# Experts' results: from row scatters by GpSimd to stores by SyncE and gathers by GpSimd

## The chip, the cores and the metric

The kernel runs on one core of a Trainium2 chip. A core has a matrix engine (TensorE, in the profile PE, with its weight loads as PEld), VectorE (DVE), ScalarE (ACT), GpSimd (POOL) and SyncE (SP); they work side by side, each through its own instructions in order, and wait for each other by semaphores. Sixteen DMA engines move data between HBM and the on-chip memory; DMAs are issued by SyncE and by GpSimd, and in this kernel only GpSimd issues those whose row addresses are data (indirect DMAs). The metric is the device time of one execution in microseconds (us). The median of three runs of the kernel before is 1285.11 us (1284.5 to 1285.67).

## The reference

The input is four sequences of 512 tokens of 256 values in float32: 2048 tokens, or 16 token tiles of 128. Four layers are added to it in turn, each with a layer norm in front: linear attention, a mixture of experts, softmax attention, and the same mixture of experts again.

```python
    x = x + _L0_attn_a_ref(_layernorm(x, axis=-1), ...)      # chunked linear attention, 16 heads
    x = x + _L0_ffn_ref(_layernorm(x, axis=-1), ...)         # experts, first use
    x = x + _L0_attn_b_ref(_layernorm(x, axis=-1), ...)      # softmax attention
    x = x + _L0_ffn_ref(_layernorm(x, axis=-1), ...)         # experts, second use

    def _L0_ffn_ref(hidden_states, gate_weight, gate_up_proj, down_proj):   # 32 experts, INTER = 96
        probs = softmax(x @ gate_weight.T)
        top_vals, top_idx = jax.lax.top_k(probs, TOP_K)                      # TOP_K = 8
        renorm = top_vals / sum(top_vals); cum = cumsum(renorm)
        num_keep = min(sum(cum < THRESHOLD) + 1, TOP_K)                      # THRESHOLD = 0.8
        ...                                                                  # combine: the kept shares, renormalised
        for each expert (w_gu, w_d, ce):
            g, u = split(x @ w_gu.T)
            acc = acc + (silu(g) * u) @ w_d.T * ce[:, None]
        return acc
```

Since seven of eight equal shares already pass 0.8, a token goes to at most seven experts (RANKS = 7).

## The kernel before

The work runs in four stages, one block of engine programs each: `lightning` (linear attention), `experts` with the name f, `attention`, and `experts` with the name g. Between two blocks every engine waits for the others. `X`, all 16 token tiles, stays on chip.

**Routing.** `Routing` picks the experts of each batch f of four token tiles. GpSimd then scatters the normalised rows into the HBM table `expert_rows`, sorted by expert: one indirect DMA of 128 rows for each token tile and rank, 28 for each batch (L981). A row has the 256 values, 32 shares (one for each expert) and 32 slot columns, which tell for each expert at which row of `result_rows` the token's result belongs (ROW = 320). `index` holds the row in `expert_rows` of each token and rank. The routing of the last batch, and its scatters, run inside `experts`.

**Experts.** 144 tiles of 128 rows, in 72 pairs. In each step u of the loop TensorE turns pair u (L1435), does gate and up of pair u-1 (L1447), turns the hidden values of pair u-2 (L1458) and does down of pair u-3 (L1466); ScalarE copies the result of pair u-4 to `ys` (`keep_result`, L1508). The pairs come in three phases of 24, 28 and 92 tiles (`PHASES`), each listed by VectorE once the batches that it covers are routed. SyncE reads the row addresses of pair u from the list (`rows_of`, L1368), waits until the ring of 8 input buffers has room, and issues two loads (L1390). In its passes 17 to 24 it also stores four rows-of-zeros tiles per pass (`store_pads`, L1399), and the first load of the last phase, pass 26, waits for all of them.

**Results.** VectorE takes the two slot columns of a pair out of its rows (L1531). GpSimd scatters the results of every pair to `result_rows`, which is in the order of the tokens, by one indirect DMA per tile (L1295). 22 pair buffers lie between ScalarE and these scatters. In stage f the last 11 pairs are scattered at the start of `attention`. SyncE loads the seven results of each of a token tile's 128 tokens by one plain DMA of 896 KB (`load`, L1304, ring of 2), and VectorE folds seven to one and adds it to `X` (`add`, L1312 and L1315). A token tile of the first two batches needs the first 44 pairs, one of the third 58, the others 65 or all 72 (`LOADED`). In f the sums of tiles 0 to 3 stand at steps 66 to 72, of tiles 4 to 15 in `attention`; in g all 16 stand from step 62 on, and each is followed by the store of the tile to the output.

What sets the order is the code itself: each engine's program is a loop over the steps with tables that say at which step a piece stands (`scatters_at`, `results_at`, `loads_at`, `adds_at`).

## Time and profile before

| what | us |
|---|---|
| median of three runs | 1285.11 |
| span of the profiled execution | 1109.5 |
| median less that span (start and end of the program, outside the trace) | 175.6 |
| `lightning` | 0 to 287 |
| `experts` f | 287 to 523.7 |
| `attention` | 523.7 to 829 |
| `experts` g | 829 to 1109.5 |
| busy: PE, DVE, ACT, POOL | 882.3, 583.1, 549.3, 647.3 |

The span runs from the first to the last instruction. A timeline row gives start, duration, engine, line, operation, and in brackets the idle time before it with what ended it. "issue" means that nothing in the profile was waited for. POOL's indirect DMAs count as busy while POOL writes their descriptors; a SyncE DMA only takes the time of its issue there, and its data land later.

### The profile page before, as it was taken

The page shows a single profiled execution, that of the slowest core. Times are in us where ns is not written, and L with a number is a line of the kernel's source. Part 1 is how long each engine was busy: PE and PEld are TensorE (multiplying, and loading weights), DVE is VectorE, ACT ScalarE, POOL GpSimd, SP SyncE. Part 2 cuts the span into 40 slices and gives each one's busy share as a digit, 9 for nine tenths or more (in the row PEclk, how much of TensorE's full clock was granted, in tenths as well). Part 3 has the DMA queues.
Part 4 walks back from the last instruction along what each step waited for, and adds up shares of the span by engine and source line. Part 5 has one row for each costly group of instructions (what it writes and reads, how often), then busy time and mean ns, then how long its engine had stood idle before and what let it go on. Part 6 is the DMA issues. An engine that isn't in the chain of part 4 may idle for free. (4 is left out here: it accounts for less than half of the span.)

```text
span 1109.5 us, 20646 instructions
## 1 busy us (share of the span) xinstructions
PE 882.3 (80%) x5504; PEld 667.1 (60%) x5504; DVE 583.1 (53%) x2104; ACT 549.3 (50%) x1088; POOL 647.3 (58%) x636
## 2 busy tenths in 40 slices
PE   5999998861588899997388987988658889999930
PEld 3666666541478799996243543534227778999830
DVE  4566785875364222226776587764623622222665
ACT  6333455730254455654267775775515454555520
POOL 2465658777666677776720011364655567777773
PEclk9999999995699999999679998988888999999975
DMA  9900002122649886783430011135327588767875
GB/s 343 381 4 2 1 25 84 72 84 82 196 163 306 285 263 219 221 268 131 144 133 34 34 34 44 44 113 212 112 104 238 188 282 276 233 217 249 288 244 195
DMA packets 93231, 181.64 MB, mean 164 GB/s; under 512 B 18985, under 2 KB 73788, under 8 KB 92736
## 3 DMA queue, kind: packets, MB, share of 16 engines
q1 hardware_dynamic: 68544, 114.19, 31.7%
q0 software_dynamic: 24576, 66.13, 16.3%
q8 instruction: 50, 0.82, 0.3%
q14 instruction: 61, 0.50, 0.2%
HBM read 96.34 MB, written 92.27 MB: 170 GB/s over the span
## 5 line engine op out<-in xcount | busy, mean ns | idle before, releaser
L1295 POOL DMA_INDIRECT result_rows<-ys,result_slots x288 | 291.5, 1012 | 104.1 <-issue 93.7
L981 POOL DMA_INDIRECT expert_rows<-route_rows,index x224 | 223.5, 998 | 99.8 <-issue 90.3
L1946 ACT ACTIVATE b_probs<-ps 128x1024 f32<-128x1024 f32 x128 | 127.8, 1031 | 43.9 <-PE ps L1795 43.3
L1447 PE MATMUL ps<-w_gu,g_xts 128*128 x576 | 109.1, 333 | 3.0 <-ACT g_xts L1490 2.2
L1447 PE MATMUL ps<-w_gu,f_xts 128*128 x576 | 108.6, 333 | 2.4 <-ACT f_xts L1490 1.9
L1447 PEld LDWEIGHTS ps<-w_gu,g_xts 128*128 128x128 f32 x576 | 94.6, 195 | 5.1 <-issue 4.9
L1447 PEld LDWEIGHTS ps<-w_gu,f_xts 128*128 128x128 f32 x576 | 94.5, 194 | 3.7 <-issue 3.6
L1540 DVE SCALAR_TENSOR_TENSOR f_h<-ps,f_xs,f_gate 128x96 f32<-128x96 f32 x144 | 39.2, 313 | 100.0 <-ACT f_gate L1497 98.5
L1540 DVE SCALAR_TENSOR_TENSOR g_h<-ps,g_xs,g_gate 128x96 f32<-128x96 f32 x144 | 39.0, 313 | 96.8 <-ACT g_gate L1497 89.6
L1807 PE MATMUL ps<-b_probs,b_v_pad 128*32 128x512 f32 x512 | 78.2, 686 | 11.4 <-issue 5.6
L1508 ACT COPY ys<-ps 128x512 f32<-128x512 f32 x144 | 83.6, 581 | 2.0 <-PE ps L1466 2.0
L1312 DVE TENSOR_TENSOR parts<-parts 128x768 f32<-128x768 f32 (+2 forms) x96 | 66.3, 691 | 16.8 <-DMA parts<-result_rows 14.5
L1466 PE MATMUL ps<-g_w_d,g_hts 128*128 x288 | 75.0, 384 | 0.0
L1466 PE MATMUL ps<-f_w_d,f_hts 128*128 x288 | 74.9, 384 | 0.0
L1795 PE MATMUL ps<-b_q_t,b_k_t 64*128 64x512 f32 x256 | 63.4, 523 | 13.0 <-ACT b_probs L1946 10.8
L1490 ACT COPY f_xts<-ps 128x512 f32<-128x512 f32 x72 | 42.2, 587 | 59.0 <-PE ps L1435 57.7
L373 PE MATMUL ps<-a_q_mask,a_k_t 128*128 128x512 f32 x128 | 67.2, 608 | 5.4 <-POOL a_q_mask L578 3.6
L1490 ACT COPY g_xts<-ps 128x512 f32<-128x512 f32 x72 | 42.2, 586 | 55.5 <-PE ps L1435 55.4
L1795 PEld LDWEIGHTS ps<-b_q_t,b_k_t 64*128 64x128 f32 x256 | 24.8, 200 | 57.6 <-issue 28.4
L1435 PE MATMUL ps<-ident,f_xs 128*128 128x128 f32 x288 | 45.4, 282 | 15.8 <-DMA f_xs<-expert_rows 15.8
L587 POOL TENSOR_TENSOR a_rrms<-a_ms,a_root 128x8 f32<-128x8 f32 x32 | 54.0, 1688 | 6.8 <-DVE a_ms L721 6.3
L578 POOL TENSOR_TENSOR a_q_mask<-a_q_t,a_head_rows 128x512 f32<-128x512 f32 x40 | 41.8, 1048 | 25.7 <-PE ps L373 21.7
(362 smaller groups left out, 1827.6 us busy)
## 6 DMA issues: line engine op xcount, KB each, us to landing
parts<-result_rows SPq DMA_DIRECT2D x32, 896.0 KB, 5.2
f_xs<-expert_rows SPq DMA_DIRECT2D x144, 160.0 KB
g_xs<-expert_rows SPq DMA_DIRECT2D x144, 160.0 KB
expert_rows<-pad_rows SPq DMA_DIRECT2D x64, 160.0 KB
w_gu<-in_Wgu SPq DMA_DIRECT2D x1, 6144.0 KB, 17.6
expert_rows<-pad_rows SPq DMA_DIRECT2D x1, 5120.0 KB, 39.7
result_rows<-ys,result_slots POOLq DMA_INDIRECT x288, 3.3
f_w_d<-in_Wdown SPq DMA_DIRECT2D x1, 4096.0 KB, 29.4
```

What stands on the lines that cost most here:

```text
L373: nc.tensor.matmul(ps[:, bank_s + q % 2, :], k_t[:, q // 2, n * P:(n + 1) * P], q_mask[:, q % 2, :, :], start=True, stop=True).then_inc(sc ...
L981: self.nc.gpsimd.indirect_dma_start(xs, bass.IndirectOffsetOnAxis(self.index[:, f, t, r:r + 1].bitcast(U32), 0), self.x_rows(f)[:, t, :], ...
L1295: self.nc.gpsimd.indirect_dma_start(self.y_dram, bass.IndirectOffsetOnAxis(self.slots[:, i, j:j + 1].bitcast(U32), 0), self.ys[:, i, j, :] ...
L1312: self.nc.vector.tensor_tensor(parts[:, 0:pairs, :], parts[:, 0:pairs, :], parts[:, left:left + pairs, :], ALU.add).then_inc(self.folded, 1)
L1447: ins = nc.tensor.matmul(ps[:, bank_gu[u % 2], j * GU:(j + 1) * GU], xts[:, u % 2, o:o + P], w_gu[:, k, bass.ds(experts[j] * GU, GU)], sta ...
L1466: ins = nc.tensor.matmul(ps[:, bank_y[u % 2], j * D:(j + 1) * D], hts[:, u % 2, j * P:(j + 1) * P], w_d[:, bass.ds(experts[j] * D, D)], st ...
L1490: nc.scalar.copy(xts[:, u % 2, :], ps[:, bank_x[u % 2], :]).then_inc(xt_sb, 1)
L1508: nc.scalar.copy(results.ys[:, results.at(u), :, :], ps[:, bank_y[u % 2], :].rearrange("p (j n) -> p j n", j=2)).then_inc(y_ready, 1)
L1540: ins = nc.vector.scalar_tensor_tensor(out=h[:, u % 2, j, 0:INTER], in0=up, scalar=share, in1=gate[:, u % 2, j, :], op0=ALU.mult, op1=ALU. ...
L1795: ins = nc.tensor.matmul(ps[:, 2 * (u % 2) + j, :], k_t[rows, g, st * P:(st + 1) * P], q_t[rows, 2 * g + jp, :], start=True, stop=True)
L1807: ins = nc.tensor.matmul(ps[j * PAD:(j + 1) * PAD, bank_values, :], v_pad[:, st, g, :], probs[:, (2 * i + j // 2) % RING, j % 2, :], start ...
L1946: nc.scalar.activation(probs[:, u % RING, :, :], ps[:, 2 * (u % 2):2 * (u % 2) + 2, :], ACT.Exp, scale=float(HD) ** -0.5).then_inc(exp_don ...
```

## The change

- The results of a pair no longer go to the token's row. SyncE stores each tile of results as a block, at the same row addresses at which it loaded the tile's input (`keep`): `result_rows` now has the rows of `expert_rows`. The registers with the addresses are kept from `load(u)` to `keep(u)`, which stands 9 passes later (BEHIND = 9). The result buffers are 4 pairs (`ys`, YS), and ScalarE waits for the store of pair u-4.
- GpSimd fetches the seven results of each token by their addresses in `index`: seven indirect DMAs of 128 rows for a token tile (`gather`), to a ring of 3 tile buffers (before: 2). A tile is gathered once its pairs are stored (`COMPLETE`, the same 44, 58, 65 and 72).
- In f tiles 0 to 7 are gathered and added inside `experts`, and tiles 8 to 15 inside `attention`, where before tiles 4 to 15 were added. In g all 16 are gathered from step 46 of GpSimd's program on, and added at steps 53 to 80 of VectorE's. The stores of the output stand behind all other work of SyncE.
- The slot columns go (ROW = 288), with the scan and the addition that filled them and the two casts per pair that read them.

```diff
-ROW = D + 2 * E
+ROW = D + E
...
-RESULTS = 22
-LATER = 11
-RESULTS_AT = PARTS_AT - RESULTS * 2 * D * 4
+PARTS = 3
...
+    def gather(self, pool, t):
+
+        if t >= self.RING:
+            pool.wait_ge(self.added, t - self.RING + 1)
+        for r in range(RANKS):
             self.nc.gpsimd.indirect_dma_start(
-                self.y_dram, bass.IndirectOffsetOnAxis(self.slots[:, i, j:j + 1].bitcast(U32), 0), self.ys[:, i, j, :],
-                None, bounds_check=NT * P * RANKS - 1, oob_is_err=False).then_inc(self.scattered[i], 16)
...
+                self.parts[:, t % self.RING, r, :].bitcast(I32), None, self.y_dram,
+                bass.IndirectOffsetOnAxis(self.index[:, t // TT, t % TT, r:r + 1].bitcast(U32), 0),
+                bounds_check=STORED - 1, oob_is_err=True).then_inc(self.gathered[t % self.RING], 16)
...
+            def keep(u):
+                sp.wait_ge(y_ready, u + 1)
+                for j, row in enumerate(held.pop(u)):
+                    sp.dma_start(results.y_dram[bass.ds(row, P), :],
+                                 ys[:, u % YS, j, :].bitcast(I32)).then_inc(results.stored[u % YS], 16)
...
-            for u in range(PAIRS + 6 * TT):
+            for u in range(PAIRS + BEHIND):
                 if u < PAIRS:
                     load(u)
                 if PADS_AT <= u < PADS_AT + E // PADS:
                     store_pads(PADS * (u - PADS_AT), PADS)
-                for t in loads_at(u):
-                    load_results(t)
+                if u >= BEHIND:
+                    keep(u - BEHIND)
...
             def keep_result(u):
                 act.wait_ge(down_ready, u + 1)
-                results.wait_free(act, u)
+                if u >= YS:
+                    act.wait_ge(results.stored[u % YS], 32 * (u // YS))
...
-                i = results.at(u)
-                for j in range(2):
-                    nc.vector.tensor_copy(results.slots[:, i, j:j + 1], xs[:, u % RING, j, bass.ds(experts[j] + D + E, 1)])
...
+        def gathers_at(slot, b):
+
+            tiles = {-1: {17: 8, 18: 9}, 0: {2: 10, 8: 11, 17: 12, 18: 13}, 1: {2: 14, 18: 15}}
...
-            sums = {-1: {9: 4, 16: 5, 26: 6, 30: 7}, 0: {1: 8, 3: 9, 13: 10, 28: 11}, 1: {13: 12, 23: 13, 27: 14, 31: 15}}
+            sums = {0: {1: 8, 3: 9, 13: 10, 28: 11}, 1: {13: 12, 23: 13, 27: 14, 31: 15}}
...
+        def gathers_at(u, last):
+
+            if u == COMPLETE[0] + 2:
+                yield from range(NT if last else 2 * TT)
...
-            first, count = (62, NT) if last else (66, TT)
-            at = u - first
-            if at >= 0 and at % 2 == 0 and at // 2 < count:
-                yield at // 2
+            for t in range(NT if last else 2 * TT):
+                if u == min(53 + 13 * t // 4, 80):
+                    yield t
```

GpSimd's program in `experts` f, before (L981 scatters the routed rows, L1295 the results; x116 is a run of 116 instructions):

```order
L981 DMA expert_rows<-route_rows,index 73728x320 x14
L1295 DMA result_rows<-ys,result_slots 14336x256 x2
L981 DMA expert_rows<-route_rows,index 73728x320 x2
L1295 DMA result_rows<-ys,result_slots 14336x256 x2
L981 DMA expert_rows<-route_rows,index 73728x320 x2
L1295 DMA result_rows<-ys,result_slots 14336x256 x2
L981 DMA expert_rows<-route_rows,index 73728x320 x30
L1295 DMA result_rows<-ys,result_slots 14336x256 x116
L1334 UNCONDITIONAL_BRANCH
```

The same place and the start of `attention` now (L976 scatters the routed rows, L1276 gathers the results, b_rrms is the root of the first batch's queries and keys):

```order
L976 DMA expert_rows<-route_rows,index 73728x288 x48
L1276 DMA parts<-result_rows,index 128x256 x56
L1313 UNCONDITIONAL_BRANCH
L68 ISA x2
L1929 UNCONDITIONAL_BRANCH
L797 MEMSET b_ln_root 128x4
L959 MEMSET g_route_root 128x4
L1952 MEMSET b_root 128x8
L816 TENSOR_TENSOR b_ln_rstd<-b_ln_var_eps,b_ln_root 128x4
L1954 MEMSET b_v_pad 128x512
L1936 TENSOR_TENSOR b_rrms<-b_mean_sq,b_root 128x8
L1276 DMA parts<-result_rows,index 128x256 x14
```

The 122 result scatters of the stage have become 56 gathers, all behind the 48 row scatters, and nothing stands between those any more.

GpSimd's start of `attention` before:

```order
L819 TENSOR_TENSOR b_ln_rstd<-b_ln_var_eps,b_ln_root 128x4
L1987 MEMSET b_v_pad 128x512
L1989 MEMSET b_v_pad 128x16
L1295 DMA result_rows<-ys,result_slots 14336x256 x14
L1969 TENSOR_TENSOR b_rrms<-b_mean_sq,b_root 128x8
L1295 DMA result_rows<-ys,result_slots 14336x256 x8
L819 TENSOR_TENSOR b_ln_rstd<-b_ln_var_eps,b_ln_root 128x4
```

Before, b_rrms stood behind 14 scatters; now it stands ahead of the first 14 gathers.

SyncE's program at the boundary between passes 17 and 18 of `experts` f, before (the last store of a tile of zeros, then the list and the loads of the next pair):

```order
L1399 DMA expert_rows<-pad_rows 128x320
L1368 TENSOR_LOAD tab
L1390 ISA
L1390 DMA f_xs<-expert_rows 128x320
L1390 ISA
L1390 DMA f_xs<-expert_rows 128x320
L1395 TENSOR_LOAD pads
```

and now (L1382 is the store of zeros, L1388 the new stores, L1348 and L1373 the list and the loads):

```order
L1382 DMA expert_rows<-pad_rows 128x288
L1388 ISA
L1388 DMA result_rows<-f_ys 128x256
L1388 ISA
L1388 DMA result_rows<-f_ys 128x256
L1348 TENSOR_LOAD tab
L1373 ISA
L1373 DMA f_xs<-expert_rows 128x288
L1373 ISA
L1373 DMA f_xs<-expert_rows 128x288
L1378 TENSOR_LOAD pads
```

Each pass of SyncE from 9 on has two more DMAs, in front of the next pair's loads.

## Rows read from the trace of the kernel before

**Rows 1.** The page: span, and busy time of each engine.
```profile
span 1109.5 us, 20646 instructions
PE 882.3 (80%) x5504; PEld 667.1 (60%) x5504; DVE 583.1 (53%) x2104; ACT 549.3 (50%) x1088; POOL 647.3 (58%) x636
```
**Rows 2.** Timeline of PE, experts f and g: start us, us, engine, line.
```profile
385.25 0.60 PE L1435 MATMUL ps<-ident,f_xs 128*128 128x128 f32 x4
...
444.54 0.60 PE L1435 MATMUL ps<-ident,f_xs 128*128 128x128 f32 x4
...
512.30 0.60 PE L1435 MATMUL ps<-ident,f_xs 128*128 128x128 f32 x4
...
518.20 1.97 PE L1466 MATMUL ps<-f_w_d,f_hts 128*128 x8
...
927.90 0.60 PE L1435 MATMUL ps<-ident,g_xs 128*128 128x128 f32 x4
...
987.19 0.60 PE L1435 MATMUL ps<-ident,g_xs 128*128 128x128 f32 x4
...
1062.46 1.99 PE L1466 MATMUL ps<-g_w_d,g_hts 128*128 x8
```
**Rows 3.** The page's costliest groups: line, what, count, busy, mean ns, idle before.
```profile
L1295 POOL DMA_INDIRECT result_rows<-ys,result_slots x288 | 291.5, 1012 | 104.1 <-issue 93.7
```
**Rows 4.** The chain that ended last, at the end of g.
```profile
1095.51 6.96 DMA parts<-result_rows
...
1104.67 0.43 DVE X L1315
```
**Rows 5.** Timeline of SP, passes 18 of f and on.
```profile
342.38 0.89 SPq L1390 DMA_DIRECT2D f_xs<-expert_rows  x2
...
378.36 21.15 SPq L1390 DMA_DIRECT2D f_xs<-expert_rows  x24
```
**Rows 6.** Timeline of SP, passes 18 of g and on.
```profile
883.01 0.89 SPq L1390 DMA_DIRECT2D g_xs<-expert_rows  x2
...
921.31 7.76 SPq L1390 DMA_DIRECT2D g_xs<-expert_rows  x10
```
**Rows 7.** DMA issues: queue, count, median us to landing.
```profile
result_rows<-ys,result_slots POOLq DMA_INDIRECT x288, 3.3
...
expert_rows<-route_rows,index POOLq DMA_INDIRECT x224, 2.5
```
**Rows 8.** Timelines of PE and ACT, one step of f.
```profile
486.89 0.60 PE L1435 MATMUL ps<-ident,f_xs 128*128 128x128 f32 x4
...
489.06 0.58 ACT L1508 COPY ys<-ps 128x512 f32<-128x512 f32 x1
```
**Rows 9.** Timeline of POOL, results' scatters at the end of g.
```profile
1077.64 1.68 POOL L1295 DMA_INDIRECT result_rows<-ys,result_slots  x1 [0.30 <-issue]
1079.63 0.97 POOL L1295 DMA_INDIRECT result_rows<-ys,result_slots  x1 [0.30 <-issue]
...
1091.79 0.97 POOL L1295 DMA_INDIRECT result_rows<-ys,result_slots  x1 [0.30 <-issue]
```
**Rows 10.** Timeline of DVE, one tile's sum at the end of g.
```profile
1077.52 2.15 DVE L1312 TENSOR_TENSOR parts<-parts 128x768 f32<-128x768 f32 x3 [1.94 <-DMA parts<-result_rows]
1079.70 0.43 DVE L1315 TENSOR_TENSOR X<-X,parts 128x256 f32<-128x256 f32 x1
```
**Rows 11.** Timeline of POOL, from experts f to attention.
```profile
523.68 0.10 POOL L800 MEMSET b_ln_root<- 128x4 f32 x1 [4.09 <-POOLq L72]
...
546.51 0.97 POOL L1295 DMA_INDIRECT result_rows<-ys,result_slots  x1 [0.30 <-issue]
547.50 1.69 POOL L1969 TENSOR_TENSOR b_rrms<-b_mean_sq,b_root 128x8 f32<-128x8 f32 x1
```
**Rows 12.** Timelines of DVE and PE, start of attention.
```profile
541.69 0.16 DVE L2041 TENSOR_SCALAR b_mean_sq<-b_ssq 128x4 f32<-128x4 f32 x1
...
549.22 1.23 DVE L2052 TENSOR_TENSOR b_raw<-b_raw,b_rrms 128x1024 f32<-128x1024 f32 x1 [2.94 <-POOL b_rrms L1969]
```
**Rows 13.** Source view of the slot casts: count, ns min/median/max, first and last start.
```profile
L1531 DVE CAST result_slots<-g_xs x144: 142/154/156, 834.0 to 1061.3; 128x1 int32 x144
```

More of the change, by code:

```diff
@@ L1265, with __init__ @@
 class Results:
-    RING = 2
+    RING = PARTS
+    STORES = 4
     FOLDS = RANKS.bit_length()
-    def __init__(self, nc, sem, X, ys, slots, parts, y_dram):
-        self.nc, self.X, self.ys, self.slots, self.parts, self.y_dram = nc, X, ys, slots, parts, y_dram
-        self.scattered = [sem(f"scattered{i}") for i in range(RESULTS)]
-        self.loaded = [sem(f"loaded{i}") for i in range(self.RING)]
+    def __init__(self, nc, sem, X, index, parts, y_dram):
+        self.nc, self.X, self.index, self.parts, self.y_dram = nc, X, index, parts, y_dram
+        self.stored = [sem(f"stored{i}") for i in range(self.STORES)]
+        self.gathered = [sem(f"gathered{i}") for i in range(self.RING)]
@@ L1332, in experts @@
     PADS = 4
-    LOADED = [COVERED[sum(t >= n for n in (2 * TT, 3 * TT, 3 * TT + TT // 2))] // 2 for t in range(NT)]
+    BEHIND = 9
+    YS = results.STORES
     with ExitStack() as ctx:
@@ L1941, in body @@
                     act.wait_ge(logits_ready, UNITS * b + u + 1)
-                    if u == 0 and first(b):
-                        results.wait_scattered(act, TILES // 2)
                     if u >= RING or not first(b):
@@ L1977, in body @@
                         routing.gpsimd(pool, step, f)
-                    for v in results_at(u, b):
-                        results.scatter(pool, v)
+                    for t in gathers_at(u, b):
+                        results.gather(pool, t)
                     for f, k in scatters_at(u, b):
@@ L1992, in _ @@
                 prepare(slot, 0)
-                for v in results_at(slot, -1):
-                    results.scatter(pool, v)
+                for t in gathers_at(slot, -1):
+                    if t == 2 * TT:
+                        results.wait_stored(pool, TILES // 2)
+                    results.gather(pool, t)
             batches(body)
@@ L2275, in program @@
                                   index)
[L2276 removed]
+                results = Results(nc, lambda n: signal(f"{use}_result_{n}"), X, index, parts, y_dram)
                 if use == "f":
```

105 lines of the change are left out of this document (26 added, 79 removed).

## The prediction

> **What bounds the kernel now.** I read the page's totals first [rows 1]: TensorE is busy 80% of the span and GpSimd 58%. That says nothing of the ends of the stages, so the chain that ended last comes next [rows 4], and then TensorE's timeline in both expert stages [rows 2]. There the reader is to see two regimes. In the steady part a step takes (512.30 - 444.54) / 24 = 2.82 us, and TensorE waits for nothing. After TensorE's last matmul of stage g, at 1062.46 + 1.99 = 1064.5, the span goes on for 45 us: GpSimd is still issuing result scatters until 1091.8 [rows 9], and the loads and sums of the token tiles follow them, up to the last sum, which ends at 1105.1 [rows 4]. So the end is set by GpSimd's queue and what hangs on it. Stage f ends in the same way: TensorE is done at 520.2, and the next stage's first instruction on GpSimd stands at 523.7, after a wait of 4.1 us [rows 2, 11].
>
> **Price of the new parts.** An indirect DMA takes GpSimd 0.97 us and 0.30 us of idle before it, 1.28 us from one to the next; 1.68 us instead of 0.97 where a sum runs beside it (one starts at 1077.52, the scatter at 1077.64) [rows 9, 10]. The trace shows only scatters, no gather. A gather writes descriptors for 128 rows as a scatter does, and scatters of two row sizes (320 and 256 columns) both land in about 3 us [rows 7]; I take 1.28 us for it. From below a gather can't be free for GpSimd; the lowest I allow is 0.5 us, half of the scatter's busy time. From above the dearest nearby row is 1.68 + 0.30 = 2 us. A token tile is then 7 x 1.28 = 8.95 us, and 0.6 us more when a sum meets it: 9.5 us. Landing of the last: 2.5 us, the smaller value of [rows 7], since it ends on chip. Fold and sum: 2.15 + 0.43, with gaps 2.65 us [rows 10].
>
> **SyncE's passes.** Two loads take 0.89 us of SyncE [rows 5]; the two stores that a pass gets are the same kind of instruction, so 0.9 us, bounded by nothing (if SyncE waited anyway) and by 1.9 us (were each as dear as a pair). A free pass takes 21.15 / 12 = 1.76 us now [rows 5] and will take 2.7 us, just under a step of 2.82. In passes 18 to 25 with their four stores of zeros SyncE is the slow one already: (378.36 - 342.38) / 7 = 5.14 us for each in f, (921.31 - 883.01) / 7 = 5.47 us in g [rows 5, 6]. Eight passes with 0.93 us more make 7.4 us. Pass 26, which opens the last phase, is that much later. There is a second path with the same start: ScalarE's copy of step s needs the store of the result four pairs back, which SyncE issues in pass s+1, and which needs some 3 us to land [rows 7]. Stepping through: the loads of pass 18 come at 343.3 in f and 883.9 in g, seven passes of 6.07 and 6.40 us lead to pass 25 at 385.8 and 928.7, its 2.7 us to pass 26 at 388.5 and 931.4, which ends 1.9 us later, at 390.4 and 933.3. Pass 27 ends 2.7 us on, and 3 us behind that the copy of step 26 may start: 396.1 and 939.0. The copy stands 2.2 us behind the start of its step (489.06 - 486.89) [rows 8]. So step 26 starts at 393.9 instead of 385.25 in f, and at 936.8 instead of 927.90 in g: +8.6 and +8.9 us [rows 2].
>
> The Trainium skill ("DMA: Bandwidth & Descriptors", section "Issuing engines are not separate DMA queues") says that issuing DMAs from another engine only saves issue time of a sequencer, usually small beside the DMA itself. By it the move to SyncE would be worth nothing and cost nothing. The rows here speak for counting SyncE's issue time in full, since a pass is at 2.7 of 2.82 us; the other reading gives the time of rival B.
>
> **When the gathers start.** The first token tile needs the first 44 pairs stored. Pair 43 is copied in step 47, and stored by SyncE in pass 52. SyncE comes out of its slow passes some three steps behind its usual place, and gains only 0.1 us in each of the 25 passes that follow. So pass 52 ends 26 passes of 2.7 us behind pass 26, and its stores land 3 us later: 390.4 + 70.2 + 3 = 463.6 in f, 933.3 + 70.2 + 3 = 1006.5 in g.
>
> **Stage f.** 56 gathers: 8 x 8.95 + 7 x 0.6 = 75.8 us, to 539.4. Landing 2.5, sum 2.65, and 0.7 to the next block: 545.3 instead of 523.7, +21.6 us. TensorE would be done at 520.2 + 8.6 = 528.8. VectorE's sums stand in steps 53 to 75, a tile in every 3.25 steps or 9.2 us, and the first would start 27 steps and 2.9 us behind step 26, at 473.0; the gathers of tile 0 land at 463.6 + 8.95 + 2.5 = 475.1. VectorE waits about 2 us at each of the first sums, behind which stand the gated products that TensorE waits for; that costs TensorE 2 us at most in all, hidden behind the gathers' end. The 122 scatters that go leave no gain in this stage, because the block waits for its last gather. What they do give, earlier row scatters of the last batch, is not on the path: the zeros of passes 17 to 24 set pass 26.
>
> **Attention.** Before, the root b_rrms stood behind 14 scatters and started at 547.50, though its input was there at 541.69 + 0.16; VectorE went on at 549.22 [rows 11, 12]. It stands ahead of the gathers now: it starts at 541.85 and is done 1.69 us later, at 543.5. That is 5.7 us earlier at the start of the stage, on the path, since VectorE waited 2.9 us for it, and a token tile's sum that stood ahead of this wait also goes. Late next is VectorE itself, with the rotation that it does meanwhile. The 14 gathers behind b_rrms take 18 us and land by 565, near the sums at slots 1 and 3; a wait there is under 1 us. The other 42 gathers of the stage stand in idle stretches of GpSimd. Twelve loads of 896 KB go too. Together -6 us.
>
> **Stage g.** From 1006.5 on: 16 x 8.95 + 15 x 0.6 = 152.2 us, then landing and sum, 5.15 us, and from the last sum to the end of the span 1109.5 - 1105.1 = 4.4 us as before [rows 1, 4]: 1168.3, +58.8 us. TensorE would be done at 1064.5 + 8.9 = 1073.4, so the reader should see about 90 us of sums and gathers with no matmul. VectorE's part, two casts of 0.154 us a pair [rows 13], is hidden behind TensorE's 2.82 us. Output stores, 16 at SyncE's end, run beside the gathers.
>
> **Sum.** +21.6 - 6 + 58.8 = +74.4 us on the span of 1109.5. What lies around the span, 1285.11 - 1109.5 = 175.6 us, stays. 1109.5 + 74.4 + 175.6 = 1359.5; I say 1359 us.
>
> **Rivals.**
> - B, SyncE's stores are hidden (it waits for the same events anyway, and the slow passes absorb them). For it: the ring of 8 input buffers is deep. Against it: in the slow passes SyncE issues without a wait, so nothing there can hide a further issue. Then gathers start 3.5 us behind the copy of pair 43: at 451 in f (444.54 + 2.2 + 0.6 + 3.5) and 993.5 in g. f ends at 532.6, +8.9; g at 993.5 + 152.2 + 9.55 = 1155.3, +45.8; with -6 the sum is +48.7: 1334 us.
> - C, a gather costs GpSimd more than a scatter: 1.6 us from one to the next. For it: each reads 128 rows from all over a table, and a scatter beside a sum took 2 us. 168 gathers are on the path (56 in f, 112 in g): 168 x 0.32 = +54 on the forecast, 1413 us. Against it: the mean over all 288 scatters is 1.01 us busy and 104.1 / 288 = 0.36 us idle, waits included [rows 3], so POOL's own work sets the pace.
> - D, SyncE becomes the bound of the steady part: a free pass takes 3.0 us instead of 2.7. 26 passes x 0.3 us x 2 stages = +15.6: 1375 us. For it: only 0.1 us is left. Against it: it needs DMAs of 0.55 us to issue.
> - E, faster than before: a gather is far cheaper for GpSimd than a scatter. At 0.5 us a tile takes 3.5 us. f ends behind TensorE, +8.6; attention -6; in g TensorE ends at 1073.4, three of the last eight tiles lie ready, the other five come 3.5 us apart behind the first sum: 1073.4 + 2.65 + 17.5 + 5.15 + 4.4 = 1103.1, -6.4. Sum -3.8: 1281 us. At 0.6 us (35 us more for each further us of a gather) it turns to no gain. For it: descriptors that end on chip might be cheaper. Against it: nothing in the rows, where size and table make no difference.
>
> **How the numbers follow.** Forecast 58% (its own range 1343 to 1375: 0.08 us for each of 168 gathers, and 1.5 us of start in each stage), B 15%, C 10%, D 10%, E 7%. The range 1324 to 1392 us holds the forecast, B, D and the cheaper end of C. A measurement of this kernel can tell some 0.2%, 2.6 us, from no change. Faster by more than that: most of E, 5%. Same: 2%. Slower: 93%.
>
> **What will show it.** Gathers 1.28 us apart, 0.6 us more beside a sum (else C or E). First gather of f at about 464; of g some 67 us before TensorE's end, and then 16 tiles of 9.5 us. SyncE's passes with zeros 6.1 us apart, and ScalarE or TensorE behind them (else B). Step 26 to 71 still 2.82 us a step (else D). b_rrms directly behind b_mean_sq. I am wrong if TensorE's end in g is again followed by less than 60 us, or if the first gather doesn't wait for a store.

## The result, and the profile after

The changed kernel takes 1351.42 us (median of 4 runs, 1347.72 to 1352.59), the one before 1285.39 us beside it; the ratio is 1.048, 95% interval 1.0435 to 1.0534 (the two medians alone give 1.051). By the medians that is 66 us slower, where 74 were forecast: 1359 us, range 1324 to 1392. The number holds. Its parts do not all hold, and one statement about the trace was wrong, so the sum came out right in part by luck, with errors that nearly cancel.

The opening of the page after, with span, busy time and share of each engine, and the row of the gathers from its list of groups:

```profile
span 1345.9 us, 20655 instructions
...
PE 940.1 (70%) x5504; PEld 703.5 (52%) x5504; DVE 540.0 (40%) x1800; ACT 548.6 (41%) x1088; POOL 591.1 (44%) x572
...
L1276 POOL DMA_INDIRECT parts<-result_rows,index x224 | 234.6, 1047 | 364.2 <-issue 350.4
```

The same two opening lines of the kernel before, from an execution taken beside the first experiment:

```profile
span 1285.2 us, 20646 instructions
...
PE 927.9 (72%) x5504; PEld 694.0 (54%) x5504; DVE 583.9 (45%) x2104; ACT 543.1 (42%) x1088; POOL 641.4 (50%) x636
```

These two executions took 1347.7 and 1286.9 us, so 1.8 and 1.7 us lie around the span, not 175.6. The trace of before that the forecast read [rows 1] shows the same instructions in 1109.5 us. It was of an execution without some 175 us that every timed execution has, and those lie inside the stages: 83 in f, 20 between the first and the last b_probs, 73 from g's first turn to the end. The tables below use the second trace.

| stretch, us | before | after | change | forecast |
|---|---|---|---|---|
| start to f's first turn of x rows | 291.7 | 289.8 | -1.9 | |
| f: first turn to the next block | 315.5 | 329.2 | +13.7 | +21.6 |
| to the first b_probs | 41.8 | 35.1 | -6.7 | -6 |
| first to last b_probs | 265.9 | 283.3 | +17.4 | |
| to g's first turn | 21.4 | 20.9 | -0.5 | |
| g: first turn to the end | 348.9 | 387.6 | +38.7 | +58.8 |
| sum | 1285.2 | 1345.9 | +60.7 | +74.4 |

(A turn is the transposing of a pair's x rows, L1435 before and L1414 after. Each value is a difference between the starts of two instructions, so the stretches add up to the span. A b_probs is ScalarE's exponential of attention's scores.)

**Where the expected signs are.** b_rrms stands at once behind its input, as foretold: it starts 17.9 us behind the stage's first memset, where before it was 23.8 [rows 11]. GpSimd's timeline after:

```profile
618.98 0.10 POOL L797 MEMSET b_ln_root<- 128x4 f32 x1 [16.14 <-POOLq L69]
...
636.84 1.74 POOL L1936 TENSOR_TENSOR b_rrms<-b_mean_sq,b_root 128x8 f32<-128x8 f32 x1 [13.73 <-DVE b_mean_sq L2010]
638.76 2.12 POOL L1276 DMA_INDIRECT parts<-result_rows,index  x1 [0.18 <-issue]
641.18 1.02 POOL L1276 DMA_INDIRECT parts<-result_rows,index  x1 [0.30 <-issue]
642.50 1.03 POOL L1276 DMA_INDIRECT parts<-result_rows,index  x1 [0.30 <-issue]
```

A gather follows the one before it after 1.32 us (1.28 forecast), so rivals C and E are out. The end of g answers to [rows 4, 9, 10], engines mixed. The last gather, its landing, and the last sum:

```profile
1329.66 1.01 POOL L1276 DMA_INDIRECT parts<-result_rows,index  x1 [0.30 <-issue]
...
1336.67 1.01 POOL L1276 DMA_INDIRECT parts<-result_rows,index  x1 [0.30 <-issue]
1339.44 2.14 DVE L1287 TENSOR_TENSOR parts<-parts 128x768 f32<-128x768 f32 x3 [6.99 <-DMA parts<-result_rows,index]
1341.62 0.42 DVE L1290 TENSOR_TENSOR X<-X,parts 128x256 f32<-128x256 f32 x1
```

VectorE waits 7 us for each of the last five tiles, and they come 9.6 us apart (9.5 forecast): the gathers bound the tail. The span goes on for 87.6 us behind the last turn of g, where it was 52.0, and for 73.7 behind TensorE's last matmul (about 90 forecast). The releaser "DMA" of the sum is its own last gather.

**What nobody expected** stands in TensorE's timeline and beside it. This is the kernel after where the gathers of g have begun (all engines, rows left out):

```profile
1163.28 1.47 PE L1426 MATMUL ps<-w_gu,g_xts 128*128 x8
...
1166.92 0.33 ACT L1476 ACTIVATE g_gate<-ps 128x192 f32<-128x192 f32 x1 [5.18 <-remote]
...
1167.45 0.54 DVE L1516 SCALAR_TENSOR_TENSOR g_h<-ps,g_xs,g_gate 128x96 f32<-128x96 f32 x2 [7.25 <-issue]
...
1169.58 0.46 PE L1437 MATMUL ps<-ident,g_h 128*128 128x128 f32 x2 [4.84 <-issue]
...
1179.00 2.92 PE L1426 MATMUL ps<-w_gu,g_xts 128*128 x8 [6.27 <-issue]
...
1188.82 4.90 SPq L1388 DMA_DIRECT2D result_rows<-g_ys  x2
...
1190.96 0.33 ACT L1476 ACTIVATE g_gate<-ps 128x192 f32<-128x192 f32 x1 [12.10 <-remote]
...
1196.39 0.66 PE L1437 MATMUL ps<-ident,g_h 128*128 128x128 f32 x2 [14.46 <-issue]
```

Every engine idles with nothing that the profile shows to wait for ("issue", "remote"), SyncE takes 4.90 us for two stores that cost it 0.89 elsewhere, and GpSimd meanwhile issues gathers unbroken. Stretches of the same trace (us, busy time and count of each engine, granted clock, DMA share, GB/s):

```profile
1150.00:1162.00 12.00, 11.80 (x75) 10.57 (x74) 2.17 (x8) 6.83 (x16) 3.05 (x3) 1.00 0.67 199
1164.00:1178.00 14.00, 3.89 (x15) 2.71 (x13) 3.05 (x6) 1.18 (x3) 10.95 (x11) 0.83 0.68 191
1178.00:1182.00 4.00, 2.92 (x8) 2.42 (x8) 0.00 (x0) 0.59 (x1) 3.08 (x4) 0.50 0.64 203
1182.00:1196.00 14.00, 0.00 (x0) 0.00 (x0) 0.54 (x2) 0.94 (x3) 10.20 (x11) 0.50 0.48 137
...
1199.00:1206.00 7.00, 7.00 (x42) 6.65 (x41) 3.61 (x9) 4.17 (x11) 0.00 (x0) 0.89 0.70 216
```

From 1182 to 1196 TensorE does nothing while GpSimd issues gathers, the last of them at 1194.23, and from 1199 on it is busy again throughout. The clock of 0.50, the lower of TensorE's two levels (1.2 GHz), follows the idle time and doubles the 1.47 us of the eight matmuls. It is a consequence, since the clock stood at 1.00 up to 1162, when the idling began. Nor is it transfer volume: 199 GB/s move where TensorE is at full pace, 137 where it stands still.

So a second ledger is needed: how much longer the 72 steps take than 2.82 us each. Pair n to m means from the turn of pair n to that of pair m+1.

| excess over 2.82 us a pair | 11 to 27 | 28 to 52 | 53 to 70 |
|---|---|---|---|
| before, f / g | 54.7 / 57.5 | 17.9 / 16.5 | 8.5 / 10.2 |
| after, f / g | 41.0 / 38.8 | 0.1 / 1.2 | 52.6 / 47.5 |

Before loses time all through a stage, after at its row scatters (pairs 12 to 15) and at its gathers (from pair 54). Not all of the first column is theirs: the first trace of before, where the engines hardly idle in this way, has 14.0 / 15.1 there, around pair 12 and at SyncE's passes with the zeros.

### The profile page after: what moved, and what is told of

Its sections match the earlier page's. It is cut to its first block and busy times, and to the rows that moved or that the text cites. A ratio compares the mean times of both kernels' runs of the same rounds, so it can differ in the third digit from the quotient of the medians.

```text
span 1345.9 us, 20655 instructions
## 1 busy us (share of the span) xinstructions
PE 940.1 (70%) x5504; PEld 703.5 (52%) x5504; DVE 540.0 (40%) x1800; ACT 548.6 (41%) x1088; POOL 591.1 (44%) x572
## 5 line engine op out<-in xcount | busy, mean ns | idle before, releaser
L1276 POOL DMA_INDIRECT parts<-result_rows,index x224 | 234.6, 1047 | 364.2 <-issue 350.4
L976 POOL DMA_INDIRECT expert_rows<-route_rows,index x224 | 224.5, 1002 | 152.9 <-issue 98.6
L1426 PE MATMUL ps<-w_gu,f_xts 128*128 x576 | 118.0, 352 | 31.0 <-issue 24.0
L1426 PE MATMUL ps<-w_gu,g_xts 128*128 x576 | 115.5, 347 | 11.7 <-issue 7.6
L1426 PEld LDWEIGHTS ps<-w_gu,f_xts 128*128 128x128 f32 x576 | 102.1, 208 | 34.9 <-issue 34.6
L1776 PE MATMUL ps<-b_probs,b_v_pad 128*32 128x512 f32 x512 | 79.6, 698 | 17.4 <-issue 10.3
L1445 PE MATMUL ps<-g_w_d,g_hts 128*128 x288 | 83.5, 417 | 2.7 <-ACT g_hts L1482 2.7
L1445 PE MATMUL ps<-f_w_d,f_hts 128*128 x288 | 81.5, 410 | 0.0
L1437 PE MATMUL ps<-ident,g_h 128*128 128x128 f32 x144 | 29.9, 291 | 56.7 <-issue 41.5
L1469 ACT COPY g_xts<-ps 128x512 f32<-128x512 f32 x72 | 42.6, 591 | 61.6 <-PE ps L1414 42.9
L1437 PE MATMUL ps<-ident,f_h 128*128 128x128 f32 x144 | 29.6, 289 | 48.6 <-issue 28.0
L1476 ACT ACTIVATE g_gate<-ps 128x192 f32<-128x192 f32 x72 | 24.1, 334 | 91.7 <-PE ps L1426 52.7
L1476 ACT ACTIVATE f_gate<-ps 128x192 f32<-128x192 f32 x72 | 24.1, 335 | 88.8 <-PE ps L1426 52.8
L1414 PE MATMUL ps<-ident,f_xs 128*128 128x128 f32 x288 | 49.0, 298 | 15.0 <-DMA f_xs<-expert_rows 15.0
## 6 DMA issues: line engine op xcount, KB each, us to landing
w_gu<-in_Wgu SPq DMA_DIRECT2D x1, 6144.0 KB, 17.9
```

Of the source, the lines that this page charges most:

```text
L976: self.nc.gpsimd.indirect_dma_start(xs, bass.IndirectOffsetOnAxis(self.index[:, f, t, r:r + 1].bitcast(U32), 0), self.x_rows(f)[:, t, :], ...
L1276: self.nc.gpsimd.indirect_dma_start(self.parts[:, t % self.RING, r, :].bitcast(I32), None, self.y_dram, bass.IndirectOffsetOnAxis(self.ind ...
L1414: ins = nc.tensor.transpose(ps[:, bank_x[u % 2], o:o + P], xs[:, u % RING, j, k * P:(k + 1) * P], ident[:, :])
L1426: ins = nc.tensor.matmul(ps[:, bank_gu[u % 2], j * GU:(j + 1) * GU], xts[:, u % 2, o:o + P], w_gu[:, k, bass.ds(experts[j] * GU, GU)], sta ...
L1437: ins = nc.tensor.transpose(ps[:, bank_h, j * P:(j + 1) * P], h[:, u % 2, j, :], ident[:, :])
L1445: ins = nc.tensor.matmul(ps[:, bank_y[u % 2], j * D:(j + 1) * D], hts[:, u % 2, j * P:(j + 1) * P], w_d[:, bass.ds(experts[j] * D, D)], st ...
```

## Experiments

The median of before was 1285 to 1304 us from one group of runs to the next, on different chips, so the ratio to before is what counts. Theory P: GpSimd's indirect DMAs hold up the other engines. Kernels that leave work out compute other values; their times are shown for what the missing part costs.

**b1_before**: the kernel before, unchanged.

> The kernel before, unchanged, profiled again. The changed kernel's median less its span is 1.8 us where the earlier profile of the kernel before left 175.6 us outside its span. If what lies around the span is the same few us for both (theory: the earlier profile caught an execution without the stretches in which the sequencers of all engines are slow), its span is about 1283 us here, with stretches in which TensorE, ScalarE, VectorE and SyncE sit idle on 'issue' while GpSimd issues indirect DMAs. If the 175.6 us really lie around the span (rival), the span is 1109 to 1112 us again.

Measured: 1287.78 us, ratio 0.999 (0.995 to 1.0029), span 1285.2 us. The first trace was the exception.

**b_noscat**: before, g's result scatters left out.

```diff
-        for j in range(2):
+        for j in range(0 if self.off else 2):
...
+                results.off = final
```

> The kernel before, with stage g's result scatters left out (GpSimd issues none of them and nothing waits for them; the sums of g take the rows of f). Theory P (GpSimd's indirect DMAs hold up the other engines, about 0.3 us per DMA when they come two to a pair): from the first to the last turn of the x rows in g 296.9 us fall to about 245 (53 steps at 2.82 in place of 3.42 and the slow ones about the 13th to 16th gone but for the row scatters' part), the time to about 1230. Rival Q (transfers' traffic or the fetching of instructions makes the steps long): they stay at 3.4 us and g at 285 to 297 us.

Measured: 1243.19 us (one run) against 1304.08; g's turns take 243.1 us, 296.9 in b1_before. From pair 15 on every step takes 2.8 us (excess of pairs 28 to 52: 0.1, in f of the same run 17.3). What is left are steps of 18.5 and 13.7 us at pairs 13 and 14, where the 28 row scatters stand. That is 54 us for 144 DMAs, of which 131 stood ahead of g's last turn in b1_before. It is as P has it, but the bytes of the scatters are gone as well, so this run alone doesn't part the two.

**a_plain**: after, each gather an ordinary GpSimd DMA of fixed rows.

```diff
-            self.nc.gpsimd.indirect_dma_start(
-                self.parts[:, t % self.RING, r, :].bitcast(I32), None, self.y_dram,
-                bass.IndirectOffsetOnAxis(self.index[:, t // TT, t % TT, r:r + 1].bitcast(U32), 0),
-                bounds_check=STORED - 1, oob_is_err=True).then_inc(self.gathered[t % self.RING], 16)
+            row = (RANKS * t + r) % E * ROOM
+            self.nc.gpsimd.dma_start(self.parts[:, t % self.RING, r, :].bitcast(I32),
+                                     self.y_dram[row:row + P, :]).then_inc(self.gathered[t % self.RING], 16)
```

> The kernel after with each of its 224 gathers an ordinary GpSimd DMA of 128 fixed rows, in the same places and with the same waits (so the sums are of the wrong rows: what is left out is the addressing by index). Theory P1 (the indirect form is what costs: 1.32 us apiece on GpSimd and the slow stretches): the DMAs follow each other in about 1 us or less, the stretches of f steps 54 to 56 and g steps 54 to 56 (26.9 us for one step after) go back to 2.8 us a step, and the time falls by 50 us or more to about 1300. Rival P2 (any DMA that GpSimd issues in a burst holds the others up): the slow steps stay as they are, and the tail changes only by the issue price. The tail with indices is 112 x 1.32 us long; with 0.9 us each it would be some 45 us shorter.

Measured: 1213.36 us, ratio 0.929 (0.927 to 0.932). GpSimd's and TensorE's rows at the first gathers of f:

```profile
506.13 1.47 PE L1425 MATMUL ps<-w_gu,f_xts 128*128 x8
...
506.63 7.66 POOL L1277 DMA_DIRECT2D parts<-result_rows  x14 [124.45 <-issue]
...
510.14 1.56 PE L1425 MATMUL ps<-w_gu,f_xts 128*128 x8 [0.24 <-issue]
...
513.29 1.56 PE L1425 MATMUL ps<-w_gu,f_xts 128*128 x8
```

Fourteen DMAs in a row, 0.55 us apiece, and TensorE goes on. Pairs 53 to 70 lose 7.5 us in f instead of 52.6, the tail behind the last turn is 45.4 instead of 87.6. Pairs 11 to 27 keep their 41 us, since the row scatters are still indirect. It is the indirect form that costs, not a burst of GpSimd's DMAs or the bytes, which are the same: P1. The plain form also is shorter to issue and reads 128 rows that lie side by side; which of these it is, no run parts.

**a_noattn**: after, the 56 gathers inside attention left out.

```diff
+        if self.skip:
+            return
...
+                    held_results.skip = True
```

> The kernel after, without the 56 gathers that GpSimd issues inside attention (the sums of f's tiles 8 to 15 take whatever lies in the buffers; the part left out is their gathering alone). In the two profiles the stretch from the first to the last b_probs is 265.9 us before and 283.3 after. Theory P (an indirect DMA that GpSimd issues holds up the other engines, some 0.3 us each): this stretch falls by 17 to about 266 us, the time from the memset of b_ln_root to the first b_probs stays at 35, the time falls to about 1334. Rival Q (the longer stretch comes of other things, the transfers' traffic or the longer program): the stretch stays at 280 to 285 and the time at 1350. Rival R (the sums wait for their gathers, and VectorE's delay is what attention feels): it would fall too, but then the profile after should show VectorE's idle time ahead of the sums of attention ended by the gathers' transfers.

Measured: 1354.13 us, ratio 1.0347 (1.0297 to 1.0398). First to last b_probs 280.9 us, which at first spoke for Q, as 283.3 had been seen. But after on this chip was not at hand. The nearest is a_ys8 (below; its eight buffers gain nothing by themselves) with 1370.98 us, ratio 1.0491 (1.0421 to 1.056), and 290.5 us from the first to the last b_probs. Against it the stretch is 9.6 us shorter and the time 11 to 19 us, by whether fast runs alone, medians or ratios are set side by side.

**a_ys8**: after, eight result buffers.

```diff
-    STORES = 4
+    STORES = 8
```

> The kernel after with eight buffers for the results of a pair in place of four. Theory B1 (in steps 22 to 27 ScalarE's copy waits for the store of the result four pairs back, which SyncE issues late because its passes with four stores of zeros last 5.24 us): those steps go back to about 2.8 us, f's turns fall from 316.6 to about 304 and g's by about as much, the time from 1351 to about 1328. Rival B2 (SyncE itself is the limit there: loads of x rows come as late as the stores, so a larger ring only moves the wait to the turn of the x rows): steps 22 to 27 stay above 3.5 us and the gain is under 5 us in all. Rival B3: the steps are won and lost again in the bursts of GpSimd's scatters, so f ends no earlier: f's gathers start by pair 56 though, so a gain in f's steps should be kept.

Measured: 1370.98 us, ratio 1.0491 (1.0421 to 1.056), no gain. In after ScalarE waited for stores at pairs 22 to 27 (engine, line, what for, total, times, longest, in 400 to 430 us):

```profile
ACT f_ys L1488 <- DMA result_rows<-f_ys: 17.6, 6, 4.1
```

With eight buffers TensorE waits for the next x rows at the same place:

```profile
410.69 0.66 PE L1414 MATMUL ps<-ident,f_xs 128*128 128x128 f32 x4 [1.64 <-DMA f_xs<-expert_rows]
...
415.97 0.66 PE L1414 MATMUL ps<-ident,f_xs 128*128 128x128 f32 x4 [1.58 <-DMA f_xs<-expert_rows]
```

One turn is 5.28 us behind the other, as far as most of SyncE's passes with four stores of zeros are apart there (5.2 to 5.3 us): B2, these passes are the limit there, and both waits only show it.

**a_again**: after, unchanged, on the chip of the next three.

> The kernel after, unchanged, on the chip that runs the next three as well, so that its stretches can be set against theirs. Theory P: the same slow places as before (28 row scatters about the 12th to 15th pair of f and g, 21 gathers about the 55th and 56th, the sevens behind it), f and g together some 628 us of turns, a ratio to before of 1.045 to 1.052. The stretch from the first to the last b_probs tells how much of the 283.3 us seen at first is its own: if the 56 gathers in attention cost nothing, it varies between runs by as much as the 10 us that it fell when they were left out.

Measured: 1365.35 us, ratio 1.048 (1.0414 to 1.0546). First to last b_probs 287.6 us. With attention's gathers (after, a_ys8, a_again, a_land, v_rows2, v_rows3) it is 278.2 to 295.8, with before's attention (b1_before, b_noscat, b_burst, v_split, v_paced) 265.9 to 277.1, in a_noattn 280.9, in a_plain 271.1. Single traces of one attention differ by up to 18 us over all chips and by up to 8 on one (a_again and a_land), so the 9.6 us by which a_noattn is under a_ys8 are no clear size. The times of the same two kernels, whose intervals don't meet, bear out P for attention: the gathers there cost something of the order of 10 us.

**a_land**: after, GpSimd waiting behind every second gather of a tile until it has landed.

```diff
+            if r % 2:
+                pool.wait_ge(self.gathered[t % self.RING], 16 * (RANKS * (t // self.RING) + r + 1))
```

> The kernel after, with GpSimd waiting behind every second gather of a tile until all gathers of that tile so far have landed; no more than three then follow one another without a pause. Theory P-burst (the other engines stop only while indirect DMAs follow one another unbroken, and a short pause lets them work on): the steps of 19 to 29 us at the 55th and 56th pair go back under 7 us each, f's turns fall from 316 to about 290 and g's by as much, although the gathers as a whole take some 244 us in g in place of 148 and the tail grows by 60 or more: time about 1390. Theory P-count (each indirect DMA costs the others a fixed time, however they are spaced, about 0.3 us in before): the 21 first gathers in after cost 45 us, so this alone would leave the steps as long. Then f and g keep their 316 and 312 us and the time goes over 1420.

Measured: 1486.89 us, ratio 1.141 (1.134 to 1.148). In f the pairs 53 to 70 lose 49.3 us, almost as much as the 55.0 of a_again, though GpSimd now pauses 2.5 to 5.3 us after two or three gathers. So P-burst's time failed. But the loss is another one. GpSimd, VectorE and TensorE in turn:

```profile
518.01 1.01 POOL L1276 DMA_INDIRECT parts<-result_rows,index  x1 [3.36 <-DMA result_rows<-f_ys]
...
521.59 2.15 DVE L1289 TENSOR_TENSOR parts<-parts 128x768 f32<-128x768 f32 x3 [15.58 <-DMA parts<-result_rows,index]
...
525.19 0.69 PE L1439 MATMUL ps<-ident,f_h 128*128 128x128 f32 x2 [14.37 <-DVE f_h L1518]
...
530.00 0.38 PE L1439 MATMUL ps<-ident,f_h 128*128 128x128 f32 x2
530.63 1.01 POOL L1276 DMA_INDIRECT parts<-result_rows,index  x1 [2.56 <-DMA parts<-result_rows,index]
531.94 1.01 POOL L1276 DMA_INDIRECT parts<-result_rows,index  x1 [0.30 <-issue]
532.82 0.38 PE L1439 MATMUL ps<-ident,f_h 128*128 128x128 f32 x2
```

In these 18 pairs TensorE waits 38.4 us for VectorE's gated products (f_h) and 0.2 us on "issue"; in a_again it was 20.4 on "issue", 22.1 for a ScalarE that idled too, and none for VectorE. VectorE in turn waits 43.2 us for gathered tiles, 1.9 in a_again: the sums stand at fixed steps of its program, ahead of the products, and the paced gathers bring a tile too late for them. While two gathers with a pause around them are issued (530.63 and 531.94) TensorE keeps its step of 2.82 us, and no two stores of SyncE take longer than 1.2 us. So the pauses do take the stops away, as P-burst has it. What they cost is a wait of VectorE that the forecast of 1390 us left out, and a tail of 173.9 us in place of 85.7.

**b_burst**: before, result scatters issued for five pairs at a time.

```diff
-                    pool.wait_ge(y_ready, v + 1)
+                    pool.wait_ge(y_ready, min(5 * (v // 5) + 5, PAIRS))
```

> The kernel before, with its result scatters issued for five pairs at a time (ten DMAs in a row when the last of the five is ready, then a pause), their number and addresses the same. Theory P-burst: each burst of 12.8 us stops the other engines for most of its length, so the turns of f and g grow by tens of us each: with five pairs at 3 to 3.4 us now and up to 20 us then, f and g would take 350 us or more each, and the time 1400 or more. Theory P-count: the same number of DMAs costs the same, g stays at 297 to 310 us and the time within 1% of before, plus up to 10 us at the end where the last burst starts late.

Measured: 1429.66 us, ratio 1.096 (1.090 to 1.103), g's turns 357.4 us. Pairs 28 to 52 have 50 or 51 scatters in both kernels. In runs of up to six (a run: less than 0.5 us idle between two; 3.0 to 3.9 on average) they cost 16 to 18 us, in runs of ten 44 to 46: 0.35 and 0.9 us each. P-count fails here, P-burst holds.

**v_split**: before, f's late scatters split 10 and 12 around b_rrms.

```diff
-                for i in slots_of(((0, 7, 1), (17, 19, 2)), slot):
+                for i in slots_of(((0, 5, 1), (17, 20, 2)), slot):
```

> The kernel before, with the 22 scatters of f's last pairs that GpSimd issues at the start of attention split 10 and 12 around b_rrms in place of 14 and 8. In the profile before b_rrms starts 23.8 us behind the memset of b_ln_root and in the one after, where nothing stands ahead of it, 17.9 us; the first b_probs follow after 41.8 and 35.1 us. Theory: b_rrms starts about 4 us earlier, the first b_probs by as much unless the last scatter, which they wait for, has become the limit (22 scatters at 1.28 us end 31 us behind the memset either way), and the time falls by 3 to 5 us, 0.2 to 0.4% under before. Rival: the wait for the last scatter is the limit already and nothing changes.

Measured: ratio 0.9998 (0.9963 to 1.0033), 12 runs. b_rrms moved 5.6 us forward, to 18.2 us behind the memset, and the first b_probs stayed at 41.8. ScalarE's row names what is late next:

```profile
652.89 1.94 ACT L1946 ACTIVATE b_probs<-ps 128x1024 f32<-128x1024 f32 x2 [4.14 <-DMA result_rows<-ys,result_slots]
```

The rival was right. It bears on the forecast too: moving b_rrms ahead was not enough by itself, the 6.7 us of after need the last scatter gone as well.

**v_rows2, v_rows3**: after with eight buffers, the 28 row scatters tied to the results copied (two, or three, for each); v_rows3 ties f's 56 gathers too.

```diff
+                    if f == B - 1:
+                        pool.wait_ge(y_ready, 9 + k // 3)
...
+                    results.gather(pool, t, (lambda k: pool.wait_ge(y_ready, min(COMPLETE[0] + 7 + k // 3, PAIRS)))
+                                   if out_rows is None else None)
```

> The kernel after with eight buffers for results (which by themselves changed nothing) and one wait more: GpSimd issues the 28 row scatters of the last quarter, which stand unbroken from about the 12th pair of a stage, two for each result that ScalarE has copied, from the 9th on. Theory P-burst (an unbroken row of scatters stops the others, a pair of them for each pair of tiles costs them 0.3 to 0.4 us each): the steps 12 to 14, which took 38 us in f and 39 in g on this chip where 8.4 would be their pace, fall by about 20 us in all in each stage after the 28 x 0.37 us that are left, and the time by some 35 us, a ratio to before of about 1.02; up to 5 us of it may be lost at pair 26, whose loads wait for the last of these scatters (due when the 23rd result is copied). Theory P-count: the same number costs the same, and the ratio stays at 1.048.

> As v_rows2, but three row scatters for each copied result (which leaves pair 26 free of waiting), and in stage f the 56 gathers too are held to three for each copied result from the 51st on, with f's sums moved to where they come in (from step 57, a tile in every 2.25 steps). Theory P-burst: steps 12 to 14 fall as in v_rows2 or a little less (3.84 us of scatters in each step are more than its 2.8); in f the steps from the 54th to the last, 102 us for 17 in place of 48 at their own pace, fall to some 80 us, since GpSimd alone needs 56 x 1.32 = 74 us. Time about 1310 to 1320 where before takes 1303. Rival: gathers stop the others by their number and not by their place (a_land pointed there: 1.1 us each with pauses as without), and only the row scatters' part is won.

Measured: v_rows2 1336.11 us, ratio 1.037 (1.032 to 1.043); v_rows3 1313.14 us, ratio 1.016 (1.012 to 1.021). Steps 12 to 14 of f, 37.8 us in a_again, are 11.0 and 10.9. But in v_rows2 the loads wait for the last row scatter and TensorE for them (7.1 us, a step of 12.7 at pair 25), and in v_rows3 ten scatters close up, from 371.81 to 383.34 us, and make a step of 11.5. So pairs 11 to 27 of f lose 34.5 and 28.7 us instead of 42.6. In v_rows3 the pairs 53 to 70 of f lose 31.1 us (55.0 in a_again), and about 8 of these come back behind the last turn (21.1 us to the next block, 12.7 before). Tied to the work that they would disturb, gathers cost 0.7 us each (46 fall there) instead of 1.0 (54). P-burst had foretold ratios of 1.02 and about 1.01, so it got the direction of both, under half of the size in v_rows2 and most of it in v_rows3.

**v_paced**: before, row scatters and held-back result scatters three for each copied result.

```diff
+                    if f == B - 1:
+                        pool.wait_ge(y_ready, 9 + k // 3)
...
-                    pool.wait_ge(y_ready, v + 1)
+                    pool.wait_ge(y_ready, v + 1 if v < 3 else max(v + 1, 18 + 2 * (v - 3) // 3))
```

> The kernel before, with two waits more on GpSimd: of the 28 row scatters of the last quarter three are issued for each result that ScalarE has copied, from the 9th on, and of the result scatters held back by them (from pair 3 on) three for each copied result from the 18th on, until they have caught up about pair 45; their number and addresses stay. In before the pairs 11 to 27 of a stage take 55 to 57 us more than 2.82 each, the pairs 28 to 52 another 17 and 53 to 70 some 10. Theory P-burst: three scatters to a step keep the steps near 3.9 us (10 us over 9 steps in v_rows3, plus about 15 us there for late loads and the zeros), so pairs 11 to 27 cost 30 to 40 us, pairs 28 to 45 some 18 and the rest 12: 10 to 25 us less in each stage, time 0.96 to 0.985 of before. Theory P-count, which before itself would then follow: the same 172 DMAs cost the same 80 us in each stage, ratio 1.00; a held-back result that comes too late for the ring of 22 would make it slower.

Measured: 1331.61 us, ratio 1.021 (1.018 to 1.025), slower. In f the pairs 11 to 27 lose 36.6 us instead of 55 to 57, as expected, but 28 to 52 lose 53.8 instead of 18, for 73 scatters that fall there instead of 51. Three scatters take GpSimd 3.84 us, more than a step, so the waits are already met when it comes to them, and the scatters close up to runs of ten and twelve. TensorE in f, beside a run of twelve (405.69 to 419.76 us):

```profile
410.14 1.47 PE L1447 MATMUL ps<-w_gu,f_xts 128*128 x8
417.02 0.66 PE L1458 MATMUL ps<-ident,f_h 128*128 128x128 f32 x2 [5.42 <-issue]
417.48 1.91 PE L1466 MATMUL ps<-f_w_d,f_hts 128*128 x4
419.18 1.06 PE L1435 MATMUL ps<-ident,f_xs 128*128 128x128 f32 x4
423.66 2.92 PE L1447 MATMUL ps<-w_gu,f_xts 128*128 x8 [3.41 <-ACT f_xts L1490]
```

No version that leaves nothing out was faster than before.

## Why the prediction was right, and where it was not

- **What lies around the span.** The step "what lies around the span, 175.6 us, stays" failed as a reading: 1.8 us lie around it. The slow stretches hid in the difference and looked like a constant. They are not the same in both kernels: pairs 11 to 70 of f and g lose 165 us before (81 and 84) and 181 after (94 and 88), in places that differ.
- **Price of a gather**: 1.32 us for 1.28. Right. A tile with its sum, 9.6 us for 9.5, too, so C and E are out. Not in the sum was what a gather costs the others: 55 us in the last 18 steps of f (a_again), 7.5 with the plain form.
- **SyncE's passes.** In part right. The two stores take 0.89 us and a free pass 2.7 to 3.0, ScalarE waits for stores at the passes with zeros, and from pair 28 to 52 a step stays at 2.8 us, so D is out. But the passes with zeros did not grow by 0.93 us, from 5.14 to 6.07 in f and from 5.47 to 6.40 in g: passes 19 to 24, behind the row scatters, take 5.5 and 5.7 us on average. Half or more of the new stores' time was absorbed there, as rival B had it; the four stores of zeros mostly take 1.93 us now, and took 1.92 to 2.74 in the first trace. Why is open. B's other half fails: pair 43 is copied at 489.8, SyncE reaches its stores in pass 52, at 496.25, as forecast, and the first gather starts at 500.22, 10.4 us behind the copy where B had 3.5. The Trainium skill ("DMA: Bandwidth & Descriptors", section "Issuing engines are not separate DMA queues") calls the issue time of a sequencer usually small relative to the DMA itself. This kernel is a case where it counts: eight DMAs make a pass of 5.2 us, and in a_ys8 TensorE waits 1.6 us for loads that SyncE issues late.
- **Start of the gathers.** 172.4 us behind f's first turn were forecast, 210.4 were found (500.22 - 289.8), and 200.0 for 172.5 in g. The pass of SyncE was right, and TensorE stood at pair 52 in both stages where the forecast implied 50 or 51. What was wrong is the length of the steps ahead of it, above all of those that the row scatters disturb: pairs 11 to 27 lose 41 us in f, and 14 in the trace that the forecast read.
- **Stage f, +21.6, measured +13.7.** The next block starts 329 us behind f's first turn where 254 were forecast, but before itself needs 315.5 and not the 232.5 of the first trace. The 56 gathers take 102.6 us (500.2 to 602.8) where 75.8 were forecast; 30 of them are pauses of GpSimd ahead of tiles 4 to 7, because the ring holds three tiles. Yet before's scatters, whose removal I put at nothing ("leave no gain in this stage"), gave some 31 us back: the excess of pairs 11 to 52 falls from 73 to 41. b_noscat shows such a gain by itself (54 us in g). This step was put at nothing because the trace it was read from had no slow stretches.
- **Attention, -6, measured -6.7 to the first b_probs, then +17.4 to the last.** The early root is right, with what v_split adds: the last scatter had to go as well. "The other 42 gathers stand in idle stretches of GpSimd" and so cost nothing is wrong: idle GpSimd is not free for others. On one chip a_noattn is 9.6 and a_plain 19.4 us shorter there than a_ys8, in one trace each, and a_noattn as a whole 11 us or more faster. The rest of the 17.4 is within what traces of one kernel differ by.
- **Stage g, +58.8, measured +38.7.** The 112 gathers took 179 us (1158.3 to 1337.7) where 152 were forecast. GpSimd sits idle 29 us ahead of tiles 4 to 9, because the ring holds three tiles, and VectorE's sums, in its program behind steps that the gathers hold up, free them late. The first gathers of tiles 4 and 5 start 1.2 us behind the end of a sum (VectorE and GpSimd, rows left out):

```profile
1204.62 0.42 DVE L1290 TENSOR_TENSOR X<-X,parts 128x256 f32<-128x256 f32 x1
...
1206.20 1.01 POOL L1276 DMA_INDIRECT parts<-result_rows,index  x1 [10.95 <-DMA result_rows<-g_ys]
...
1217.94 0.42 DVE L1290 TENSOR_TENSOR X<-X,parts 128x256 f32<-128x256 f32 x1
...
1219.51 1.01 POOL L1276 DMA_INDIRECT parts<-result_rows,index  x1 [4.38 <-issue]
```

  Against this, before's own g lost 84 us, of which the first trace showed 17 and most of the rest goes to its scatters, and after only 40 up to its first gather. So the gathers of g, forecast to start 67 us before TensorE's end, started 114 us before it.
- **The sum.** +60.7 between the two traces, 66 between the medians. The slow stretches of before were missing from the stages of the base (but were in the 175.6 us), and those of after from the terms. That the two are nearly equal, 165 and 181 us, was luck, and without it the number would not have come out.

## What to carry to other kernels

Compare the profiled span with the timed median before any ledger: a gap of 14% is not start-up until a second trace says so. Count indirect DMAs on GpSimd twice, once for their own time and once for what they take from all other engines, and never call them hidden because GpSimd is idle; where they can't be avoided, issue at most as many for each step as fit well inside it, tied by a semaphore to the pipeline's own progress, and move the work that needs their data back by as much, since an engine whose program waits for a late tile holds up all that stands behind it (a_land). A wait inserted for pacing does nothing when the paced engine needs longer for its share than the step lasts.

## What the runs showed of the hardware

- Indirect DMAs on GpSimd hold up TensorE, ScalarE, VectorE and SyncE, at 0.35 us of TensorE's time each in runs of up to six, 0.9 in runs of ten, 1.0 for gathers in runs of 28 and 7. Where GpSimd pauses 2.5 us or more after two or three gathers, TensorE stands on "issue" for 0.2 us in 18 steps instead of 20 to 30. Ordinary GpSimd DMAs, 0.55 us apiece and 14 in a row, cost about 0.15 us each (7.5 us for 51). The Trainium skill ("DMA: Bandwidth & Descriptors", section "SWDGE vs HWDGE vs iDMA") says that DMAs issued by SyncE or ScalarE are immune to the interference that GpSimd's descriptor writing meets with VectorE. No run here tests that interference, but SyncE's issue is slower beside GpSimd's indirect DMAs: 4.90 us for two stores, 0.89 without.
- Open: which shared resource it is; whether a gather without any stop beside it would still cost the others something (in a_land the waits of VectorE cover it); and why the first trace of before ran the same instructions without it.
